# A 64-graph network in straight form, with the division later and GpSimd making three hidden units of each slot

## What is computed

```python
hi = jnp.einsum('bsh,hk->bsk', x, W1[:H])
hj = jnp.einsum('bsh,hk->bsk', x, W1[H:])
h = jax.nn.relu(hi[:, :, None, :] + hj[:, None, :, :] + b1)
y = jnp.einsum('bijk,kl->bijl', h, W2) + b2
y = _layernorm(y, gamma, beta)
out = jnp.einsum('bij,bijh->bih', adj, y)
...
x = _layernorm(x + _L0_gnn_ref(x, adj, ...), axis=-1)
x = _layernorm(x + _L1_gnn_ref(x, adj, L1_gnn_W, L1_gnn_b), axis=-1)
x = _layernorm(x + _L2_gnn_ref(x, adj, nodemask, ...), axis=-1)
x = _layernorm(x + _L3_gnn_ref(x, adj, ...), axis=-1)
```

## Time and profile before

| | us |
|---|---|
| median of 3 runs (3005.57 to 3007.0) | 3005.89 |
| the profiled execution | 3005.84 |
| its span, first to last instruction | 3004.1 |
| TensorE busy | 2807.9 (93%) |
| ScalarE busy | 2838.4 (94%) |
| VectorE busy | 2746.3 (91%) |
| GpSimd busy | 436.1 (15%) |

### The profile page before, as it was taken

One profiled execution on the slowest core, in us unless ns is written; L12 is line 12 of the kernel. 1 busy time (PEld: TensorE's weight loads), 2 busy tenths in 40 slices (PEclk: granted clock), 3 DMA queues, 4 the chain that ended last, 5 costly groups with the idle time before them and its releaser, 6 DMA issues.

```text
span 3004.1 us, 68152 instructions
## 1 busy us (share of the span) xinstructions
PE 2807.9 (93%) x10882; PEld 1136.5 (38%) x10882; DVE 2746.3 (91%) x21521; ACT 2838.4 (94%) x8004; POOL 436.1 (15%) x978
## 2 busy tenths in 40 slices
PE   8999999999999999999999999999999999999994
PEld 2333333334333343343343333433333333334332
DVE  4999998999989999898998989989899898999997
ACT  8999999999999999999999999999999999999992
POOL 0011111111111111111111111111111111111111
PEclk9999999999999999999999999999999999999996
DMA  3455454545544554454444544544454454445542
GB/s 120 197 198 217 178 210 186 196 181 204 208 180 179 213 200 178 180 219 194 179 197 195 200 177 192 221 180 180 179 228 184 177 210 189 193 182 200 211 179 118
DMA packets 170281, 571.44 MB, mean 190 GB/s; under 512 B 68608, under 2 KB 104320, under 8 KB 104320
## 3 DMA queue, kind: packets, MB, share of 16 engines
q1 hardware_dynamic: 169856, 567.82, 48.2%
HBM read 555.17 MB, written 8.39 MB: 188 GB/s over the span
## 4 chain that ended last, share of the span: by engine, by line
ACT 47%; PE 25%; issue 14%; DVE 6%; DMA 4%; SPq 4%; ACTq 0%; POOL 0%; DVEq 0%; POOLq 0%
ACT h L521 27%; PE y_ps L383 16%; ACT sq L531 13%; PE ss_ps L395 4%; DMA devs<-dev_rows 4%; SPq L300 4%; DVE h L644 3%; ACT dev_rows L538 2%; ACT aggT L556 1%; DVE h L630 1%; PE prod_bank L416 1%; ACT aggT L564 1%; DVE gT L644 1%; ACT h L569 1%; ACT xT L503 1%
## 5 line engine op out<-in xcount | busy, mean ns | idle before, releaser
L383 PE MATMUL y_ps<-h,w2c 128*128 128x512 f32 x4096 | 2092.6, 622 | 143.6 <-DVE h L630 131.6
L644 DVE CUSTOM_DVE_ANT_0 h<-h,cb 128x128 f32<-128x128 f32 x8192 | 1921.2, 280 | 47.2 <-issue 35.7
L521 ACT ACTIVATE h<-uv_ps,uT 128x128 f32<-128x128 f32 x5760 | 1922.4, 695 | 18.7 <-DVE gT L644 18.7
L531 ACT ACTIVATE sq<-y_ps,b2c_col 128x1024 f32<-128x1024 f32 x1024 | 1441.1, 1407 | 82.2 <-PE y_ps L383 78.1
L383 PEld LDWEIGHTS y_ps<-h,w2c 128*128 128x128 f32 x4096 | 665.4, 190 | 1139.8 <-issue 670.1
L644 DVE DVE_READ_ACCUMULATOR2_ANT gT<- 128x1 f32 x8192 | 641.5, 78 | 0.0
L395 PE MATMUL ss_ps<-sq,sel 128*32 128x512 f32 x4096 | 549.2, 608 | 1.1 <-ACT sq L531 1.0
L630 DVE TENSOR_SCALAR h<-vT,uT 128x128 f32<-128x128 f32 x2176 | 508.3, 276 | 14.8 <-issue 7.6
L871 POOL TENSOR_TENSOR var_eps<-mv,eps_col 128x1 f32<-128x1 f32 x448 | 85.9, 192 | 2034.9 <-DVE mv L671 2034.9
L874 POOL TENSOR_TENSOR rs<-var_eps,minus_half 128x1 f32<-128x1 f32 x448 | 306.6, 684 | 35.0
L395 PEld LDWEIGHTS ss_ps<-sq,sel 128*32 128x32 f32 x4096 | 81.7, 108 | 250.7 <-issue 152.6
(11 more groups left out here) (99 smaller groups left out, 1530.5 us busy)
## 6 DMA issues: line engine op xcount, KB each, us to landing
cb<-c_scratch SPq DMA_DIRECT2D x512, 1024.0 KB, 8.0
adj_c<-in_adj_dram SPq DMA_DIRECT2D x512, 8.0 KB
devs<-dev_rows SPq DMA_DIRECT2D x512, 8.0 KB
x_in<-in_x_dram SPq DMA_DIRECT2D x64, 64.0 KB, 10.5
c_scratch<-c SPq DMA_DIRECT2D x128, 32.0 KB, 1.4
adj_in<-in_adj_dram SPq DMA_DIRECT2D x64, 64.0 KB, 2.7
x_res<-in_x_dram SPq DMA_DIRECT2D x64, 64.0 KB, 4.4
out_dram<-x SPq DMA_DIRECT2D x64, 64.0 KB, 2.0
```

The costliest lines, as they stand in the source:

```text
L383: op = pe.matmul(y_ps[:, t % 2, c0:c0 + COLS], w2c[:], h[:, t, c0:c0 + COLS], start=True, stop=True)
L521: op = act.activation(h[:, t, n * P:(n + 1) * P], v, ACT.Relu, bias=uT[:, b, i:i + 1])
L531: act.activation(sq[:, t % SQ_RING, :], y_ps[:, t % 2, :], ACT.Square, bias=b2c_col[:], scale=float(P) ** -0.5).then_inc(sq_done, 1)
L644: op = dve.tensor_tensor_reduce(h[:, t, cols], h[:, t, cols], cb[:, t // 2, c0:c0 + P], 1.0, 0.0, ALU.mult, ALU.add, gT[:, i:i + 1])
```

## The change

It does four things. The loop is gone: all 67 iterations are written out in straight form. GpSimd makes units 0 to 2 of each slot (POOL_UNITS), in front of its other steps of the slot; VectorE makes one unit of a graph (unit 3 of the last slot), ScalarE units 3 to 7 (4 to 7 in the last slot). The reciprocal and the coefficients move on VectorE from fine steps 5 and 6 of their slot to steps 0 and 2 of the next. l0_sum, ln0 and x1_scaled are placed two, two and one fine steps later. TensorE waits for the new semaphore h_pool at the head of each slot, and for h_dve in the last slot only.

```diff
-UNROLL = 4
+POOL_UNITS = 3
...
 def vector_units(t):
-    if t == SLOTS - 1:
-        return BLOCK_UNITS
-    return 2
+    return BLOCK_UNITS - POOL_UNITS if t == SLOTS - 1 else 0
...
-    ("g_keep", 2, 4), ("l0_mm", 3, 0), ("l0_sum", 3, 3), ("ln0", 3, 4), ("x1_scaled", 4, 5),
+    ("g_keep", 2, 4), ("l0_mm", 3, 0), ("l0_sum", 3, 5), ("ln0", 3, 6), ("x1_scaled", 4, 6),
...
-            first = 4 + (G - 5) % UNROLL
-            for i in range(first):
+            for i in range(G - 1):
                 iteration(i + 1, about(i), i % 2)
-            with eng.Fori(0, (G - 1 - first) // UNROLL) as rounds:
-                for n in range(UNROLL):
-                    g = UNROLL * rounds + (first + n)
-                    iteration(g + 1, (g, g - 1, g - 2, g - 3), (first + n) % 2)
...
                 if block_of_duo == 0:
-                    wait(pe, h_dve, SLOTS * g + t + 1)
+                    wait(pe, h_pool, SLOTS * g + t + 1)
                     if t < SLOTS - 1:
                         wait(pe, h_act_head, (SLOTS - 1) * g + t + 1)
+                    else:
+                        wait(pe, h_dve, g + 1)
...
-                if n == vector_units(t):
+                if n == POOL_UNITS + vector_units(t):
                     wait(act, ttr_done, SLOTS * (g - 1) + t + 1)
...
                     for k in range(FINE):
+                        if ct % HALF == 1 and cg is not None and k == 0:
+                            invert(cg, ct // HALF)
+                        if ct % HALF == 1 and cg is not None and k == 2:
+                            coefficients(cg, ct // HALF)
...
-                        if ct % HALF == 0 and cg is not None and k == 5:
-                            invert(cg, ct // HALF)
-                        if ct % HALF == 0 and cg is not None and k == 6:
-                            coefficients(cg, ct // HALF)
...
+            def hidden(g, b, t, n):
+                if n == 0:
+                    wait(pool, ttr_done, SLOTS * (g - 1) + t + 1)
+                    if t == 0:
+                        wait(pool, uv_ready, g + 1)
+                i = unit_of(t, n)
+                op = pool.tensor_scalar(h[:, t, n * P:(n + 1) * P], vT[:, b, :], uT[:, b, i:i + 1], 0.0, ALU.add, ALU.max)
+                if n == POOL_UNITS - 1:
+                    op.then_inc(h_pool, 1)
+
             def iteration(after, graphs, buf):
                 for s in range(SLOTS):
+                    hg, ht = lagging(graphs, s, START)
+                    hb = buf if s >= START else 1 - buf
+                    if hg is not None:
+                        for n in range(POOL_UNITS):
+                            hidden(hg, hb, ht, n)
```

More of the change, by code:

```diff
@@ L171, in build @@
             sem("x_in_in"), sem("x_turned"), sem("xT_set"), sem("uv_made"), sem("uv_ready"))
-        h_dve, h_act_head, h_act = sem("h_dve"), sem("h_act_head"), sem("h_act")
+        h_dve, h_pool, h_act_head, h_act = sem("h_dve"), sem("h_pool"), sem("h_act_head"), sem("h_act")
         y_done, sq_done = sem("y_done"), sem("sq_done")
@@ L507, in keep_uv @@
                 wait(act, uv_made, g + 1)
-                wait(act, h_dve, SLOTS * (g - 1))
+                wait(act, h_dve, g - 1)
+                wait(act, h_pool, SLOTS * (g - 1))
                 wait(act, h_act, SLOTS * (g - 1))
@@ L601, in iteration @@
                     tail_steps(1, 4)
-                    first = vector_units(ht)
+                    first = POOL_UNITS + vector_units(ht)
                     for n in range(first, DUO_UNITS):
@@ L622, in hidden @@
             def hidden(g, b, t, n):
-                if n == 0:
+                if n == POOL_UNITS:
                     wait(dve, ttr_done, SLOTS * (g - 1) + t + 1)
-                    if t == 0:
-                        wait(dve, uv_ready, g + 1)
+                    wait(dve, uv_ready, g + 1)
                 i = unit_of(t, n)
                 op = dve.tensor_scalar(h[:, t, n * P:(n + 1) * P], vT[:, b, :], uT[:, b, i:i + 1], 0.0, ALU.add, ALU.max)
-                if n == vector_units(t) - 1:
+                if n == POOL_UNITS + vector_units(t) - 1:
                     op.then_inc(h_dve, 1)
@@ L810, in iteration @@
                     for k in range(FINE):
+                        if ct % HALF == 1 and cg is not None and k == 0:
+                            invert(cg, ct // HALF)
+                        if ct % HALF == 1 and cg is not None and k == 2:
+                            coefficients(cg, ct // HALF)
                         if k == BLOCK_UNITS:
                             if hg is not None:
-                                for n in range(vector_units(ht)):
+                                for n in range(POOL_UNITS, POOL_UNITS + vector_units(ht)):
                                     hidden(hg, hb, ht, n)
@@ L820, in iteration @@
                             later_layers(g, b, place + k, place + k + 1)
-                        if ct % HALF == 0 and cg is not None and k == 5:
-                            invert(cg, ct // HALF)
-                        if ct % HALF == 0 and cg is not None and k == 6:
-                            coefficients(cg, ct // HALF)
-                        if ct == HALF and cg is not None and k == FINE - 1:
+                        if ct == HALF + 1 and cg is not None and k == FINE - 1:
                             wait(dve, c_made, 2 * (cg + 1))
```

## The result

The changed kernel takes 3054.42 us (median of 4 runs, 3051.55 to 3055.9) against 3005.82 before: a ratio of 1.016, interval 1.0142 to 1.0177. It is 1.6% slower, where I forecast 2837 us, 5.6% faster.

The account below looks back on a forecast made before the run. ScalarE was taken to pace the ordinary 44.77 us iteration, busy for 44.22. From a span of 3004.1, 67 for the loop and 102 (65 by 1.57) came off: 2835, or 2837 us with what lies around it; range 2720 to 3100.

Parts of the forecast that it names:

- The loop goes: -67: Returns of the hardware loop: 13 returns by 5.15 us, 67.0 us saved, with -62 to -72 as ends.
- ScalarE 40.5, VectorE 42.4, TensorE 41: Work per iteration after the change, in us; VectorE's is 36.2 plus 6.2 for GpSimd's units.
- GpSimd's own price: 0.30 to 0.43 us a unit: GpSimd's queue: 48 units a graph are 14 to 21 us, with norms and some waiting under 32 of some 43.
- What GpSimd's units cost VectorE: 0.13: VectorE's weighted sums beside GpSimd's units: 0.13 us lost a unit, 48 of them 6.2 us; ends 0 and 0.29.
- my 43.2: Forecast iteration: VectorE's 42.4 us plus a margin of 0.8, 1.57 less than 44.77.
- The division moved: VectorE's reciprocal and coefficients: made at about the same time, no transfer behind them later by more than a few tenths.
- The units come late: Rival, GpSimd's queue: units made after the norms, TensorE waits for h, iteration stays at 44.8; 2939 us, chance 0.11.
- The lock on VectorE, my slower rival: Rival, VectorE's queue behind each GpSimd unit: 0.24 us a unit, threshold 0.183, iteration 48.5; 3181 us, chance 0.28.

Follow-up runs that it names:

- the last run above: Changed kernel with two units of a slot on GpSimd, one on VectorE, five on ScalarE, and the set-up moved: 2778.9 us, 0.9248 of before.
- the reduction: Changed kernel with VectorE's weighted sums replaced by plain sums over h by tensor_reduce, coefficients left out: 2793.64 us, 0.9289 of before.
- The probe: Kernel before plus six GpSimd instruction forms on own tiles, at 128 and 512 columns; unit's form 0.71 and 2.02 us in the set-up.
- the straight kernel with the later steps: Changed kernel with no unit on GpSimd, VectorE two of a slot, ScalarE six; straight form and later division stay: 2914.9 us, 0.9697 of before.
- them put back: Straight kernel without GpSimd units, with reciprocal, coefficients, l0_sum, ln0 and x1_scaled where they stood before the change: 2913.1 us, 0.9689 of before.

## Why the prediction was wrong

I forecast 5.6% faster, and it is 1.6% slower. That 3054 lies inside my range, 2720 to 3100, is luck: the upper end stood for VectorE held up by 0.21 us a unit, which did not happen.

- **The loop goes: -67.** Right in sign, and the 13 returns right in size; measured 93.7 us in all, since the other iterations of the loop shortened too.
- **ScalarE 40.5, VectorE 42.4, TensorE 41.** Near: ScalarE is at 41.56 in the changed kernel and 40.6 in the last run above, VectorE at 40.0. TensorE, where it is busy throughout, takes 41.55 (the reduction); I had counted some 18 small products, but a graph has 42 (10882 / 64 - 128).
- **GpSimd's own price: 0.30 to 0.43 us a unit, "GpSimd is no bound by its sum".** This is the step that failed. I put the unit on a line through a cast (0.82 ns a column) and, as an upper end, a subtraction of two tensors (1.88), because all three seemed of one kind. The probe shows 3.4 ns for this form, 0.69 to 0.71 us at 128 columns. 48 of them are 33 us by themselves, and my upper end of 21 did not take it in. GpSimd is busy for 44.9 us of an iteration where I had it under 32. The Trainium skill ("GPSIMD Engine Reference", Engine selection) calls one-input operations on GpSimd roughly line-rate. The copy's 0.75 ns a column does not speak against that; the unit's 3.4, with one tensor input too, does.
- **What GpSimd's units cost VectorE: 0.13.** Measured 0.08 a unit. The range of 0 to 0.29 held it, but I had charged one side only. In the same sentence in which I read that GpSimd gives way by 0.13 us, I left that loss out of GpSimd's sum: 48 by 0.11 to 0.14 is 5 to 7 us an iteration. Neither error would have been enough by itself: with the loss alone GpSimd comes to some 35 us at most; 33 and the norms' 6.3 are 39.4 us, still under my 43.2, and the run with the reduction, where the loss is gone, takes 2794 us. The own price and the loss together carried GpSimd over ScalarE and TensorE.
- **The set-up in front of the units.** Not in my working at all: I checked what stands around the units in the steady queue and not what stands ahead of the first one. The cost is 14 us.
- **The division moved: nothing.** Right that nothing would be lost; nothing was won either. VectorE's wait for the deviations did not go with the move: it is 103.7 us in the straight kernel with the later steps and 103.2 with them put back (56.1 in the changed kernel, of which 50.3 are one wait).
- **The rivals.** None was this one. "The units come late" had the engine and the waiter right (its sign was a wait of over 50 us by TensorE for GpSimd's h, and its matmuls waited 189.6) but blamed the order of the queue and priced it as no loss. The lock on VectorE, my slower rival, didn't happen at its price of 0.183 us a unit or more: 0.08 was measured.

The account: 3004.1 before. The straight form takes the span to 2909.0. The start adds 14. The interval grows from 44.28 (without GpSimd's units) to 46.36, 2.08 by the 59 later ones are 123. Together 3046; the intervals in the first few iterations and the close, each some us longer, are the rest to 3053.7. Against my 43.2 us an interval of 46.36 is 3.16 too long, and 59 by 3.16 is 186 of the 217 us between forecast and result.

## What to carry to other kernels

Before work goes to an idle engine, price it there in the very form that it will have, scalars and number of operations included; neighbours of another form were off by a factor of two to four per column here. Charge a meeting of two engines to both sides, and sum the receiving engine's queue with the loss in it. And look at what stands in its queue ahead of the first moved instruction.

## What the runs showed of the hardware

- GpSimd, float32, from 128 to 512 columns (the probe): copy 0.75 ns a column, addition of two tensors 1.7, add and max with scalars 3.4.
- Which side pays in a meeting was not the same in any two cases: the unit's form of 0.69 us lost 0.23 us beside unbroken weighted sums and cost VectorE 0.08; the addition of two tensors lost 0.03 to 0.05 and cost VectorE about 0.19 at each meeting; beside VectorE's tensor_scalar in place the unit lost 0.38; the same form with 512 columns beside VectorE's hidden units lost 0.04 and cost VectorE 0.6; beside a reduction the unit lost nothing that can be seen. What decides it is open.
- A return of the hardware loop stopped VectorE for 2.86 us of "issue" and lengthened the iteration by about 5.15 us; the other iterations inside the loop took some 0.4 us more than the same work written out.
